# Taking out the products of the identity that TensorE does at the end of a recurrent scan

## The chip, the cores and the metric

The kernel runs on one core of a Trainium2 chip. The metric is the device time of one execution in microseconds (us); several executions are timed and their median is taken. One further execution is recorded by the hardware profiler. Times inside it are counted from the start of its span. Only the time is at stake: the change touches nothing that reaches the output.

## The reference

Two layers act on 32 sequences of 192 tokens (64 image patches and 128 text tokens) with 256 channels. Layer 0 is an embedding, causal attention and a feed-forward block with ternary weights. Layer 1 begins with a gated linear recurrence and ends with a small mixture of experts. The recurrence, cut to its core (h has 512 channels, one state for each sequence):

```python
xi, z = jnp.split(x @ Win.T, 2, axis=-1)
lam = jnp.exp(-8 * softplus(omega) * sigmoid(xi @ Wl.T + bl))
v = xi @ Wv.T + bv
def step(h_prev, inp):
    x_t, v_t, lam_t = inp
    vh = jnp.sum(v_t * h_prev, axis=-1, keepdims=True)
    vv = jnp.sum(v_t * v_t, axis=-1, keepdims=True)
    h = lam_t * (h_prev - 2.0 * v_t * (vh / vv)) + (1.0 - lam_t) * x_t
    return (h, h)
out = (silu(z) * h) @ Wout.T
```

The expert block works on 512 tokens: for each of 8 experts a 256 to 512 product, a gated activation, a 256 to 256 product and a weighted sum.

## The kernel before, in words

The program is three blocks one after the other on one core: part A (layer 0), part B (the recurrence) and part C (the experts). Between two blocks all engines meet.

Part B cuts the 192 time steps into TT = 48 tiles of four steps. Its loop runs over i from -5 to 50, and every engine has its own copy of it. In pass i the four scan steps of tile i are done (t = 4i + k, k from 0 to 3), and between them the engines work on other tiles: projections of tile i + 3, the layer norm of tile i + 5, the transposes and the output product of tile i - 1, the residual sum of tile i - 2. For i of 45 and more there are no projections left.

One scan step is a ring between two engines. VectorE (DVE) forms the products of v and the state and their sum over a partition's channels (L1219). TensorE (PE) adds these partial sums over the partitions of a sequence, with one matrix product of one column, which I call the dot (L1329, two records for each). Meanwhile VectorE multiplies the state by the decay (L1221) and adds the drive (L1224). Then it adds the dot times `B_decayed_u` (L1235), and the next step's products follow. The scan's state lives in PSUM.

TensorE's queue in pass i is: dot 0; for tiles 44 and 45 ("parted") the last nine products of `wout` (L1342, output of tile i - 2); projections; dot 1; transposes of the normalised rows of tile i + 4 (L1369, two); transposes of `B_y` of tile i - 1 (L1378, four); dot 2; projections; dot 3; `wout` of tile i - 1 (12 products, or the first three of a parted tile). The queue is in order. The transposes at L1369 wait until VectorE has done the residual sum of tile i - 2 (L1247), which needs that tile's whole `wout`.

After tile 47's scan come ScalarE's (ACT) copy of the states (L1139), GpSimd's (POOL) product with the gate (L1050), the transposes at L1378, ScalarE's L1166, VectorE's L1279, tile 47's `wout` and residual sum L1247. Then ScalarE sends four rows by a DMA, and the block ends.

Part C opens on TensorE with four transposes of the routing weights (L1603), half of expert 0's first product (`gate_up(0, ...)`, 24 products, L1573), the products of the biases (L1609, eight records) and two transposes of the last normalised rows (L1614). ScalarE and VectorE split the result (L1489, L1519), and only then can the rest of `gate_up(0)` and everything behind it go.

The identity products that the change takes out are written into TensorE's queue at two places: six after each dot of tiles 45, 46 and 47, and ten at the end of the block. They write to a PSUM bank whose contents nobody reads any more.

Of the kernel before, what the change touches and what calls it, by code (L numbers as in the profile page):

```python
# [26 lines left out]
P = 128  # L27
# [820 lines left out]
def part_b(nc, W, E, io, consts):  # L848
    TT = T // 4
    R_RES, R_RING = 12, 4  # L850
    SQRT_HALF = 0.5 ** 0.5
    with ExitStack() as ctx:
# [3 lines left out]
        ident, ones, halfpow = consts.ident, consts.ones, consts.halfpow  # L856
# [33 lines left out]
        ps = W.ps  # L890
# [4 lines left out]
        def bank(what, j):  # L895
            return (4 * j + "l v xi z".split().index(what)) % 3
# [10 lines left out]
        s = {}  # L907
# [22 lines left out]
        def products(t):  # L930
            return 4 * t + 1
# [10 lines left out]
        def has(j):  # L942
            return 0 <= j < TT
# [359 lines left out]
        def _(pe):  # L1303
# [18 lines left out]
            def step(i, k):  # L1322
                if not has(i):
                    return
                t = 4 * i + k
                if t == 0:
                    pe.wait_ge(s["minus_zero"], 8)
                pe.wait_ge(s["scan"], products(t))
                nc.tensor.matmul(dot[:, t % 2:t % 2 + 1], minus[:], part[:, t % 2:t % 2 + 1], start=True,  # L1329
                                 stop=True).then_inc(s["dot"], 1)  # L1330
                if i >= TT - 3:

                    pe.wait_ge(s["u"], TT)
                    for _ in range(6):
                        nc.tensor.transpose(ps[:, bank("v", TT - 1), 0:P], ident[:], ident[:])

            def wout(j, first, stop):
                terms = [t for g in range(IC) for t in ((y_h[:, j % 2, g, :], out_h[:, g, :]),
                                                        (y_h[:, j % 2, g, :], out_l[:, g, :]),
                                                        (y_l[:, j % 2, g, :], out_h[:, g, :]))]  # L1340
                for n in range(first, stop):
                    last = nc.tensor.matmul(ps[:, OUT, 0:D], *terms[n], start=(n == 0), stop=(n == len(terms) - 1))  # L1342
                if stop == len(terms):
                    last.then_inc(s["wout"], 1)


            parted = (TT - 4, TT - 3)
            for i in range(FIRST, LAST):
                step(i, 0)
                if i - 2 in parted:  # L1350
                    wout(i - 2, 3, 3 * IC)
                if has(i + 3):
                    j = i + 3
                    pe.wait_ge(s["x_lo"], j + 1)
                    pe.wait_ge(s["bias_l"], j + 1)
                    project(ps[:, bank("l", j), :], j, l_h, l_l, biased=True).then_inc(s["l"], 1)
                step(i, 1)
                if has(i + 3):
                    j = i + 3
# [13 lines left out]
                if has(i - 1):  # L1373
# [3 lines left out]
                    for r in range(4):  # L1377
                        last = nc.tensor.transpose(ps[:, TURN, :].rearrange("p (a r) -> p r a", r=4)[:, r, :],  # L1378
                                                   y[:, j % 2, r, :], ident[:])
                    last.then_inc(s["yT"], 1)  # L1380
                step(i, 2)
                if has(i + 3):
                    j = i + 3
# [11 lines left out]
                if has(i - 1):  # L1395
# [3 lines left out]
                    pe.wait_ge(s["y_lo"], j + 1)  # L1399
                    wait(pe, s["x_lo"], min(i + 5, TT + 3))  # L1400
                    wout(j, 0, 3 if j in parted else 3 * IC)
            for _ in range(10):
                nc.tensor.transpose(ps[:, bank("v", TT - 1), 0:P], ident[:], ident[:])


def part_c(nc, E, io, consts):
# [318 lines left out]
```

## Time and profile before

| | |
|---|---|
| median of 3 runs | 981.53 us (979.28 to 981.59) |
| the profiled execution: its time | 979.7 us |
| its span, first to last instruction | 977.8 us |
| mean granted TensorE clock | 0.993 |
| TensorE busy | 934.9 us, 96% of the span |
| VectorE busy | 791.8 us, 81% |
| ScalarE, GpSimd busy | 594.2 us, 545.2 us |
| part B's scan | 483 to 893 us |
| part C | from 901.35 us |

The profiled execution is within the runs. Its time is 1.9 us above its span. A clock of 1.00 is 2.4 GHz and 0.50 is 1.2 GHz. Matrix products are pipelined, so the time from one product's start to the next says more than a product's own duration.

### The profile page before, as it was taken

To read this page: it belongs to the slowest core of one execution; us is meant where nothing else is said; L and a number is where in the kernel's file an instruction comes from. 1 tells how busy PE (TensorE), PEld (TensorE's weight loads), DVE (VectorE), ACT (ScalarE), POOL (GpSimd) and SP (SyncE) were. 2 spreads that over 40 slices of the span, in tenths; PEclk is the share of its full clock that TensorE was granted. 3 is DMA by queue.
4 is the path that set the end of the run, shared out by engine and by line. 5 is a ranking of instruction groups with operands and counts; after the bars stand their busy time and mean duration, and the time that the engine had idled before them with its cause. 6 is when DMAs were issued, how large, how long until landed. Compare 5 with 4: busy or idle time off the path is not lost. (4 is left out here: it accounts for less than half of the span.)

```text
span 977.8 us, 19833 instructions
## 1 busy us (share of the span) xinstructions
PE 934.9 (96%) x6016; PEld 837.6 (86%) x6016; DVE 791.8 (81%) x2376; ACT 594.2 (61%) x1183; POOL 545.2 (56%) x675
## 2 busy tenths in 40 slices
PE   6889999999999999988899999999999999998998
PEld 6789999999999999875678888888888888877887
DVE  4878877777778777774589999999999989995787
ACT  1366666666666666664666767667767766752442
POOL 4256666666666666444445545455455456552673
PEclk9999999999999999999999999999999999999999
DMA  6001111111111113003799899999999999992310
GB/s 226 17 28 44 45 44 44 43 43 43 43 43 43 43 57 128 17 17 113 94 146 153 151 155 158 153 151 152 167 153 173 180 166 154 153 140 52 121 65 22
DMA packets 63014, 96.35 MB, mean 99 GB/s; under 512 B 12366, under 2 KB 32982, under 8 KB 62294
## 3 DMA queue, kind: packets, MB, share of 16 engines
q1 hardware_dynamic: 61390, 91.19, 50.1%
q0 software_dynamic: 1536, 4.20, 1.5%
q8 instruction: 37, 0.61, 0.3%
q14 instruction: 43, 0.35, 0.2%
q10 hardware_dynamic: 8, 0.00, 0.0%
HBM read 31.91 MB, written 13.11 MB: 46 GB/s over the span
## 5 line engine op out<-in xcount | busy, mean ns | idle before, releaser
L334 POOL TENSOR_TENSOR gelu_lo<-gelu_out,gelu_hi 128x384 fp32r<-128x384 f32 x124 | 146.0, 1205 | 29.2 <-DVE gelu_hi L549 28.7
L1050 POOL TENSOR_TENSOR B_y<-B_scan_in,B_states 128x512 f32<-128x512 f32 x48 | 61.8, 1288 | 84.8 <-ACT B_states L1139 84.8
L752 PE MATMUL psAB<-ternary_down,gelu_hi 128*128 128x256 f32 x384 | 96.9, 291 | 5.3 <-POOL gelu_lo L334 4.5
L688 PE MATMUL psAB<-x2T_hi,ternary_up 128*128 128x384 f32 x256 | 92.7, 362 | 0.8 <-DVE residual L678 0.6
L752 PE MATMUL psAB<-ternary_down,gelu_lo 128*128 128x256 f32 x384 | 93.4, 282 | 0.0
L688 PE MATMUL psAB<-x2T_lo,ternary_up 128*128 128x384 f32 x256 | 86.1, 336 | 0.0
L1317 PE MATMUL psAB<-Win_hi,B_x_hi 128*128 128x512 f32 x192 | 83.5, 435 | 0.0
L752 PEld LDWEIGHTS psAB<-ternary_down,gelu_hi 128*128 128x128 f32 x384 | 72.2, 188 | 9.7 <-POOL gelu_lo L334 8.0
L1062 POOL TENSOR_TENSOR B_decayed_u<-B_scan_in 128x512 f32<-128x512 f32 x48 | 62.1, 1293 | 29.5 <-DMA B_scan_in<-B_stage 28.2
L1235 DVE SCALAR_TENSOR_TENSOR psAB<-B_decayed_u,psAB 128x128 f32<-128x128 f32 x192 | 67.8, 353 | 12.1 <-PE psAB L1329 11.2
L1329 PEld LDWEIGHTS psAB<-B_partial_dots,B_minus_same_batch 128*128 128x128 f32 x384 | 65.3, 191 | 14.3 <-DVE B_partial_dots L1219 4.1
L1317 PE MATMUL psAB<-Win_hi,B_x_lo 128*128 128x512 f32 x192 | 75.5, 393 | 0.0
L1317 PE MATMUL psAB<-Win_lo,B_x_hi 128*128 128x512 f32 x192 | 75.3, 392 | 0.0
L752 PEld LDWEIGHTS psAB<-ternary_down,gelu_lo 128*128 128x128 f32 x384 | 72.5, 189 | 0.0
L1056 POOL TENSOR_TENSOR B_v_scale<-B_half_vv,half_powers 128x1 f32<-128x1 f32 x48 | 26.3, 549 | 78.8 <-ACT B_v_squared L1160 78.8
L403 ACT ACTIVATE gelu_out<-psAB 128x384 f32<-128x384 f32 x128 | 62.7, 490 | 10.2 <-PE psAB L688 9.9
L1219 DVE CUSTOM_DVE_ANT_0 B_products<-B_scan_in,psAB 128x128 f32<-128x128 f32 x192 | 55.2, 287 | 13.4 <-DVE psAB L1235 8.0
L1224 DVE TENSOR_TENSOR psAB<-psAB,B_scan_in 128x128 f32<-128x128 f32 x192 | 57.5, 299 | 6.5
L568 DVE TENSOR_TENSOR gelu_sq_sum<-gelu_sq_sum,gelu_sq 128x384 f32<-128x384 f32 x105 | 61.2, 582 | 1.7
L1329 PE MATMUL psAB<-B_partial_dots,B_minus_same_batch 128*128 128x1 f32 x384 | 54.8, 212 | 3.9 <-DVE B_partial_dots L1219 3.6
L1342 PE MATMUL psAB<-Wout_hi,B_y_hi 128*128 128x256 f32 x192 | 55.6, 290 | 2.7 <-DVE B_y_lo L1279 1.5
L390 ACT ACTIVATE gelu_sq<-gelu_out 128x384 f32<-128x384 f32 x112 | 57.3, 528 | 0.0
(274 smaller groups left out, 3318.2 us busy)
## 6 DMA issues: line engine op xcount, KB each, us to landing
B_scan_in<-B_stage SPq DMA_DIRECT2D x192, 256.0 KB, 6.9
patches<-in_patches SPq DMA_DIRECT2D x16, 384.0 KB, 3.1
B_residual<-layer_out SPq DMA_DIRECT2D x48, 128.0 KB, 4.1
out_dram<-B_residual SPq DMA_DIRECT2D x48, 128.0 KB, 3.7
layer_out<-residual SPq DMA_DIRECT2D x32, 128.0 KB, 1.8
raw_Win<-in_experts SPq DMA_DIRECT2D x3, 768.0 KB, 4.2
raw_Wl<-in_experts SPq DMA_DIRECT2D x3, 768.0 KB, 4.2
layer_out<-residual SPq DMA_DIRECT2D x32, 64.0 KB, 2.0
```

The costliest lines, as they stand in the source:

```text
L334: nc.gpsimd.tensor_tensor(act_l[:, k, :], act[:, k % DEEP, :], act_h[:, k, :].bitcast(F32), ALU.subtract).then_inc(s["ffn_lo"], 1)
L390: nc.scalar.activation(out, act[:, k % DEEP, :], ACT.Square).then_inc(s["sq_done"], 1)
L403: nc.scalar.activation(act[:, k % DEEP, :], ps[:, 6 + k % 2, 0:GT], ACT.Gelu).then_inc(s["gelu_done"], 1)
L568: nc.vector.tensor_tensor(sqsum[:], sqsum[:], sq[:, k % DEEP, :], ALU.add).then_inc(s["sqsum_done"], 1)
L688: last = nc.tensor.matmul(out, a, b, start=(n == 0), stop=(n == len(terms) - 1))
L752: last = nc.tensor.matmul(ps[:, 6 + k // 2, (k % 2) * D:(k % 2 + 1) * D], x[:, c, k * P:(k + 1) * P], dn_w[:, c, :], start=(c == 0 and x i ...
L1050: nc.gpsimd.tensor_tensor(y[:, j % 2], ring[:, j % R_RING, :, GATE, :], hs[:, j % 2], ALU.mult).then_inc(s["y"], 1)
L1062: nc.gpsimd.tensor_tensor(lu[:, j % 2], ring[:, j % R_RING, :, LAM, :], ring[:, j % R_RING, :, U, :], ALU.mult).then_inc(s["lu"], 1)
L1224: nc.vector.tensor_tensor(state(j, k), state(j, k), ring[:, j % R_RING, k, DRIVE, :], ALU.subtract).then_inc(s["scan"], 1)
L1235: nc.vector.scalar_tensor_tensor(out=state(i, k), in0=lu[:, i % 2, k, :], scalar=dot[:, t % 2:t % 2 + 1], in1=state(i, k), op0=ALU.mult, o ...
L1317: last = nc.tensor.matmul(out, a, b, start=(not biased and ks[0] == 0 and n == 0), stop=(ks[-1] == DC - 1 and n == len(terms) - 1), skip_g ...
L1329: nc.tensor.matmul(dot[:, t % 2:t % 2 + 1], minus[:], part[:, t % 2:t % 2 + 1], start=True, stop=True).then_inc(s["dot"], 1)
```

## The change

The six identity products after each scan dot of the last three tiles are removed, 72 in all, with the wait ahead of them, and so are the ten that end the block. Nothing is put in their place. VectorE's, ScalarE's, GpSimd's and SyncE's programs are unchanged.

```diff
                 pe.wait_ge(s["scan"], products(t))
                 nc.tensor.matmul(dot[:, t % 2:t % 2 + 1], minus[:], part[:, t % 2:t % 2 + 1], start=True,
                                  stop=True).then_inc(s["dot"], 1)
-                if i >= TT - 3:
-
-                    pe.wait_ge(s["u"], TT)
-                    for _ in range(6):
-                        nc.tensor.transpose(ps[:, bank("v", TT - 1), 0:P], ident[:], ident[:])
...
                     wout(j, 0, 3 if j in parted else 3 * IC)
-            for _ in range(10):
-                nc.tensor.transpose(ps[:, bank("v", TT - 1), 0:P], ident[:], ident[:])
```

## Rows read from the trace of the kernel before

**Rows 1.** The page: span, busy time of engines, granted clock in 40 slices.

```profile
span 977.8 us, 19833 instructions
PE 934.9 (96%) x6016; PEld 837.6 (86%) x6016; DVE 791.8 (81%) x2376; ACT 594.2 (61%) x1183; POOL 545.2 (56%) x675
PEclk9999999999999999999999999999999999999999
```

**Rows 2.** Chain that ended last, part C's opening: start us, us, what.

```profile
901.39 0.60 PE psC L1603 x4
901.99 2.87 PE psC L1573 x24
904.86 1.92 PE psC L1609 x8
906.78 0.38 PE psC L1614 x2
...
907.60 0.44 DVE Wl_Win_lo L1519
```

**Rows 3.** Windows from:to: length, busy us by engine, granted clock, DMA.

```profile
53.30:56.60 3.30, 3.03 (x14) 3.03 (x15) 2.02 (x9) 1.45 (x4) 0.00 (x0) 0.50 0.00 0
490.10:493.50 3.40, 1.79 (x9) 1.18 (x8) 2.47 (x10) 2.65 (x6) 2.28 (x4) 1.00 1.06 136
493.60:496.90 3.30, 3.30 (x11) 2.62 (x10) 2.52 (x8) 1.55 (x3) 1.41 (x2) 0.50 1.06 138
...
875.80:879.20 3.40, 2.30 (x18) 1.66 (x15) 3.09 (x14) 0.09 (x1) 2.47 (x5) 1.00 1.08 175
879.30:882.60 3.30, 3.30 (x18) 3.30 (x17) 1.28 (x7) 0.90 (x2) 1.28 (x1) 0.50 1.05 132
882.70:886.10 3.40, 3.26 (x29) 2.90 (x28) 3.05 (x12) 0.87 (x2) 1.28 (x1) 1.00 0.14 42
886.10:889.50 3.40, 2.89 (x25) 2.60 (x24) 2.66 (x12) 0.60 (x1) 1.29 (x1) 1.00 0.02 5
```

**Rows 4.** Source view of L1335: duration ns min/median/max, first and last start.

```profile
L1335 PE MATMUL psAB<-ident x72: 272/273/421, 872.0 to 892.7; 128*128 128x128 f32 x72
```

**Rows 5.** TensorE's timeline in the stretch of the change: start us, us, instruction.

```profile
879.17 1.47 PE L1335 MATMUL psAB<-ident 128*128 128x128 f32 x6
880.29 0.56 PE L1342 MATMUL psAB<-Wout_hi,B_y_hi 128*128 128x256 f32 x1
...
881.93 0.41 PE L1342 MATMUL psAB<-Wout_lo,B_y_hi 128*128 128x256 f32 x1
882.14 0.41 PE L1342 MATMUL psAB<-Wout_hi,B_y_lo 128*128 128x256 f32 x1
...
883.33 0.38 PE L1369 MATMUL psAB<-ident,B_normed 128*128 128x128 f32 x2
...
883.99 0.28 PE L1329 MATMUL psAB<-B_partial_dots,B_minus_same_batch 128*128 128x1 f32 x2
...
895.34 0.63 PE L1378 MATMUL psAB<-ident,B_y 128*128 128x128 f32 x4 [0.67 <-POOL B_y L1050]
...
898.95 1.25 PE L1403 MATMUL psAB<-ident 128*128 128x128 f32 x10
```

**Rows 6.** VectorE's timeline there; in brackets idle time and its releaser.

```profile
882.60 0.42 DVE L1247 SCALAR_TENSOR_TENSOR B_residual<-psAB,B_residual 128x256 f32<-128x256 f32 x1 [1.86 <-PE psAB L1342]
...
889.52 0.42 DVE L1247 SCALAR_TENSOR_TENSOR B_residual<-psAB,B_residual 128x256 f32<-128x256 f32 x1 [0.39 <-PE psAB L1342]
...
891.12 0.36 DVE L1235 SCALAR_TENSOR_TENSOR psAB<-B_decayed_u,psAB 128x128 f32<-128x128 f32 x1
```

**Rows 7.** Timelines of GpSimd and ScalarE at the end of part B and after.

```profile
893.92 1.28 POOL L1050 TENSOR_TENSOR B_y<-B_scan_in,B_states 128x512 f32<-128x512 f32 x1 [4.44 <-ACT B_states L1139]
```

```profile
899.61 1.19 ACTq L1193 DMA_DIRECT2D raw_Wv<-B_residual  x1
...
904.80 0.60 ACT L1486 ACTIVATE C_normed<-raw_Wv,C_shift,C_rstd 128x256 f32<-128x256 f32 x1 [1.94 <-POOL C_shift L1465]
```

## The prediction

> **What bounds the kernel now.** I read the page first: TensorE is busy for 96% of the span, VectorE for 81%, and the granted clock shows nines all the way [rows 1]. Taken alone this says that TensorE is the bound and that 82 fewer products are a gain. So I went on to the stretch of the change, 871.9 to 901.3 us. All 72 identity products after the dots lie there [rows 4], and the ten of the end start at 898.95 [rows 5].
>
> In that stretch no projections are left, and the scan's ring sets the pace. VectorE's timeline shows it at work except where it waits for `wout`: 1.86 us ahead of 882.60 and 0.39 us ahead of 889.52 [rows 6]. In between, an identity product mostly fills time in which TensorE would wait for VectorE's products.
>
> Then I read the chain that ended last. It reaches back to TensorE's opening of part C: four transposes, 24 products in 2.87 us, the biases in 1.92 us, two transposes, and VectorE's split at 907.60 [rows 2]. `C_normed` was there at 904.80 + 0.60 = 905.4 [rows 7], but its transposes stand in TensorE's queue behind the biases and start only at 906.78. So part C's opening is bound by TensorE, and each microsecond lost there goes straight into the end: the rest of `gate_up(0)`, and through it VectorE, ScalarE and GpSimd, begin from that split.
>
> Last I read the granted clock in windows. It is not always full. It is 0.50, that is 1.2 GHz, from 53.3, from 493.6 and from 879.3 us, each time for about 3.4 us (a fourth such spell is in part A's start). Ahead of them TensorE had little to do (1.79 us of 3.40 ahead of 493.6), in them it worked without a pause (3.30 of 3.30 at 879.3), and then the clock was full again [rows 3]. At 879.3 it fell although identities were in the queue: 875.8 to 879.2 has only 18 products in 2.30 us [rows 3]. Later, from 882.7 to 886.1, hardly anything but identities, other transposes and dots ran (29 products, 3.26 us), and the clock stayed at 1.00 in the next window too [rows 3]. So what the identities do to the time goes by two ways: the place that they take in the queue, and the clock.
>
> TensorE: Matmul & The Clock Gate, a page of the Trainium skill, says in its Part 4 (PE-mode transpose) that the full clock does not engage for transposes, since they do not count as busy time in the same way. By that rule the identities hold nothing up, and the sum below would be that of the third rival. The trace disagrees, by the two windows just named.
>
> **The change part by part.** In the new kernel TensorE has, from 871.9 us on, only dots, six transposes a tile and `wout`. I expect the clock to fall some microseconds earlier than 879.3, to come back only after the dense pieces (`wout`), and to fall again in each gap. The price of the low level: `wout`'s products start 0.21 us apart (881.93 to 882.14) [rows 5], against 2.87 / 24 = 0.12 us at full clock [rows 2]. A microsecond of dense work at the low level loses 1 - 0.12/0.215 = 0.45 us.
>
> Term 1, tile 46, step 0. Six identities stand ahead of the nine products of `wout` for tile 44, from 879.17 to 880.29 [rows 5], 1.12 us, while VectorE waits 1.86 us for the last of them [rows 6]. The nine ran at the low clock before and will after: 1.12 us gained. Ends: 1.86 us if the clock is full, 0 if something else is late. I take -1.1.
>
> Term 2, tile 46, steps 1 and 2. The residual sum now starts at 881.5 and ends at 881.9, and six transposes follow. At the low clock they take 6 x 0.215 = 1.3 us, and the dot behind them starts at 883.25 instead of 883.99 [rows 5]. The lead is 0.75 us instead of 1.1, and less by the dot's own slowness. So +0.5, between 0 (full clock) and 0.7.
>
> Term 3, tile 47, step 0. Before, six identities (0.72 us at 0.12 each) and nine products (1.06 us) lay between dot and residual sum, 1.78 us. After, nine at 0.215: 1.93 us. +0.15; ends -0.4 (the whole wait of 0.39 [rows 6]) and +0.2.
>
> Term 4, dots at the low clock. In most steps other work of VectorE covers the dot. In four steps of tiles 46 and 47 nothing lies between the drive and L1235, as at 891.12 [rows 6]. A pair of dot records takes 0.28 to 0.38 us at full clock; doubled it would cost up to 0.38 a step, nothing at the least. No row shows an uncovered dot at the low level. I take 0.1 in each of the four, +0.4, nearer the low end since a part falls at full clock; ends 0 and 1.5.
>
> Terms 1 to 4: -1.1 + 0.5 + 0.15 + 0.4 = -0.05. The scan ends where it did, which is the first point of the forecast: the identities' place in the queue and the clock cancel.
>
> Term 5, the end of part B. Tile 46's `wout` starts near 892.9: 12 products at 0.215 are 2.6 us, to 895.5. `B_y` is ready at 893.92 + 1.28 = 895.20 [rows 7] and its transposes started at 895.34 [rows 5], so 0.1 us is lost, and four slow transposes lose 4 x 0.1. Tile 47's `wout`, after this dense piece, should find the clock full. +0.5; ends 0, and 1.7 if its 12 products are low too (12 x 0.1 more).
>
> Term 6, the ten identities of the end. They run from 898.95 to 900.2 under ScalarE's issue of the DMA, 899.61 to 900.80 [rows 5, 7]. Their place is worth nothing. What they may do is hold the clock. Without them TensorE has nothing from 899.2 to 901.4, after 12 products (1.4 us) and an earlier gap of 1.5 us; the low level followed stretches with as little work as that [rows 3].
>
> Term 7, part C's opening at the low clock. The spells seen ended after some 3.4 us of dense work [rows 3]. Counted from 901.4 this gives 3.4 us, and the rise may come earlier or somewhat later by where the fall lay. I take 4.2 us x 0.45 = +1.9. Ends: 0 if the clock is full, and 24 x 0.095 + 1.92 + 0.3 = 4.5 if the products, the biases (twice their time) and the transposes all run low. I take a value nearer the middle since every spell in the rows ended by itself under dense work.
>
> Sum: -0.05 + 0.5 + 1.9 = +2.4 us. On the profiled execution 979.7 + 2.4 = 982.1. The median of the runs stands 1.8 us above that execution; the same difference on the median gives 981.5 + 2.4 = 983.9 us, or 0.24% slower.
>
> **The rivals.**
>
> First, low throughout. The clock doesn't come back before the split of part C. Term 5 becomes 1.7, term 7 becomes 4.5, the dots cost a little more: +6, 987.5 us. For it: the work from 886 to 901 is in short pieces. Against it: every low spell in the trace ended under dense work [rows 3], and 24 products in a row are dense. It decides if no rise is seen before the biases at L1609. A milder form, one spell more than I count, gives +4.
>
> Second, full clock in part C. The two `wout`s and the transposes from 892.9 on keep the clock up over the gap. Terms 1 to 5 stand, term 7 is 0: +0.5, 982.0 us. For it: in the rows the clock falls only after a stretch of little work, not at once. Against it: the gap of over 2 us follows another of 1.5 us.
>
> Third, not slower at all: the identities don't hold the clock, and only their place in the queue goes. The clock stays as before, with one low spell near 879. Gains: 1.1 at tile 46, 0.4 at tile 47 and some 0.3 of late dots, -1.8, 979.7 us (-2.7 if the spell misses `wout` as well). For it: the fall at 879.3 in spite of them. Against it: windows of identities alone, at full clock. It decides if the mean clock from 871.9 to 901.3 is no lower than before.
>
> **How the numbers follow.** The forecast case, clock low in pieces and in the opening of part C, has 0.60, with its own range +1.2 to +4.0, 982.7 to 985.5. Low throughout or one spell more: 0.15. Full clock in part C: 0.16. No hold on the clock: 0.09. The range of 980.5 to 986.5 takes in the forecast, the second rival, half of the first and some of the third. A change of 0.3%, 2.9 us, is about what a measurement of this kernel can tell. Slower by more: the upper part of the forecast case (0.29) and the first rival, 0.44. Faster by more than that needs more than the queue's place can give, 0.06. Within: 0.50.
>
> **What would show each step.** In the windows, the granted clock below 1.00 in at least two more pieces between 872 and 901, and 0.50 at the start of part C, returning before the biases end; the 24 products of its opening taking some 4.7 us instead of 2.87. VectorE's wait for `wout` in tile 46 about 0.8 instead of 1.86. The last L1235 of the scan within 0.6 us of 892.86, and part C starting 0 to 1 us later. I would be wrong if the 24 products took 2.9 us, if the scan ended over 1 us earlier or later, or if the delay at part C's split were absorbed further on.

## The result, and the profile after

| | before | changed |
|---|---|---|
| median of 7 runs each | 981.59 us (979.28 to 984.45) | 986.95 us (984.59 to 990.41) |
| profiled execution, its span | 979.7, 977.8 us | 986.9, 985.0 us |
| mean granted clock there | 0.993 | 0.977 |
| part C starts | 901.35 us | 906.12 us |

The ratio is 1.0057, 95% interval 1.0036 to 1.0077: the changed kernel is 5.4 us slower, just outside the range of 980.5 to 986.5. I forecast 983.9.

The page's clock line now shows a hole where before there were nines only [rows 1]; PE's instructions are 82 fewer and its busy time is the same.

```profile
PE 935.2 (95%) x5934; PEld 839.4 (85%) x5934; DVE 791.0 (80%) x2376; ACT 595.2 (60%) x1183; POOL 544.9 (55%) x675
PEclk9999999999999999999999999999999999975999
```

The windows of the changed kernel's trace (length, busy time and count of PE, PEld, DVE, ACT, POOL, then the granted clock) answer to [rows 3]:

```profile
871.90:876.50 4.60, 3.14 (x23) 2.77 (x24) 4.11 (x15) 1.66 (x3) 2.26 (x5) 1.00 1.07 129
876.60:881.60 5.00, 2.93 (x14) 2.50 (x13) 4.62 (x20) 1.08 (x3) 1.48 (x2) 0.50 1.07 163
881.70:886.20 4.50, 4.11 (x20) 4.02 (x20) 2.66 (x11) 0.95 (x3) 2.18 (x4) 0.50 0.97 142
886.30:891.80 5.50, 3.72 (x16) 3.67 (x17) 4.32 (x17) 1.31 (x3) 2.55 (x2) 0.50 0.02 4
891.90:895.60 3.70, 2.41 (x11) 1.90 (x10) 3.19 (x13) 0.60 (x1) 0.00 (x0) 0.50 0.11 35
895.70:899.50 3.80, 3.79 (x16) 3.38 (x16) 0.65 (x2) 0.60 (x1) 1.28 (x1) 0.50 0.02 4
899.60:903.80 4.20, 2.84 (x12) 2.63 (x12) 0.69 (x1) 2.07 (x3) 0.00 (x0) 0.50 0.22 61
903.90:907.20 3.30, 1.03 (x10) 0.99 (x10) 0.82 (x2) 1.05 (x1) 0.00 (x0) 1.00 0.01 2
907.30:910.60 3.30, 3.30 (x18) 3.30 (x17) 0.70 (x3) 0.94 (x2) 2.25 (x5) 0.50 0.83 256
...
914.20:917.40 3.20, 3.05 (x14) 3.05 (x15) 0.92 (x3) 1.59 (x2) 2.12 (x1) 0.50 0.58 230
```

From 876.6 to 903.9 us the clock is at 1.2 GHz without a break, 27.3 us. Neither the nine products of `wout` from 881.7 on (TensorE busy for 4.11 of 4.50 us) nor the 12 and four transposes from 895.7 on (3.79 of 3.80 us) brought it back. It came back at 903.9, behind tile 47's last 12, fell again at 907.3 in part C's opening and once more at 914.1, behind the split. The chain that ended last shows what that did to the opening [rows 2], 24 products in 4.36 us instead of 2.87:

```profile
906.17 0.60 PE psC L1596 x4
906.77 4.36 PE psC L1566 x24
911.13 1.92 PE psC L1602 x8
913.04 0.38 PE psC L1607 x2
...
913.87 0.43 DVE Wl_Win_lo L1512
```

VectorE's timeline, with idle time and its releaser in brackets, answers to [rows 6]:

```profile
883.96 0.42 DVE L1247 SCALAR_TENSOR_TENSOR B_residual<-psAB,B_residual 128x256 f32<-128x256 f32 x1 [0.80 <-PE psAB L1337]
...
886.36 0.36 DVE L1235 SCALAR_TENSOR_TENSOR psAB<-B_decayed_u,psAB 128x128 f32<-128x128 f32 x1 [0.84 <-PE psAB L1329]
...
892.06 0.42 DVE L1247 SCALAR_TENSOR_TENSOR B_residual<-psAB,B_residual 128x256 f32<-128x256 f32 x1 [0.80 <-PE psAB L1337]
...
893.83 0.36 DVE L1235 SCALAR_TENSOR_TENSOR psAB<-B_decayed_u,psAB 128x128 f32<-128x128 f32 x1 [0.20 <-PE psAB L1329]
...
903.93 0.42 DVE L1247 SCALAR_TENSOR_TENSOR B_residual<-psAB,B_residual 128x256 f32<-128x256 f32 x1 [3.02 <-PE psAB L1337]
```

The waits for the parted output are 0.80 us each, where they were 1.86 and 0.39.

To compare executions I cut each profile at four of VectorE's instructions: the last gate product (L1253, tile 45), the last L1235 of the scan, the last residual sum (L1247), and part C's split. The difference in span is 7.2 us. Of this, 2.3 us had arisen before the first cut (873.72 to 875.99), where both kernels run the same code; that part is how far one execution differs from another, here with the same 10.2 us of low clock ahead of the cut in both. Behind the cut it is 4.9 us, near the 5.4 us of the medians. "Low" is the time at 1.2 GHz between the first cut and the split of that one profile. "Low, timed" is the median over the timed runs, for the whole execution, worked out from each run's mean clock as 2 x (1 - clock) x span. All columns but the last two are single profiles; ratios are those of the timed runs to the kernel before on the same chip.

| run | scan | end of B | C's opening | rest | low | low, timed | ratio (95% interval) |
|---|---|---|---|---|---|---|---|
| before | 19.14 | 6.29 | 8.45 | 70.20 | 3.4 | 14 to 16 | 1 |
| changed | 19.58 | 8.36 | 9.94 | 71.13 | 30.7 | 41 | 1.0057 (1.0036 to 1.0077) |
| e1_drop_ten | 17.57 | 6.31 | 8.44 | 70.23 | 0 | 16 | 1.0009 (0.999 to 1.0027) |
| e2_keep_ten | 19.28 | 7.11 | 8.45 | 70.23 | 17.1 | 35 | 1.0034 (1.0016 to 1.0051) |
| e3_thin | 24.46 | 7.71 | 9.94 | 71.16 | 30.7 | 52 | 1.0123 (1.01 to 1.0146) |
| e4_fit | 16.55 | 6.31 | 8.46 | 71.06 | 0 | 17 | 1.0003 (0.9985 to 1.0022) |
| e5_end_only | 19.57 | 8.00 | 8.47 | 70.17 | 23.9 | 33 | 1.0038 (1.002 to 1.0056) |
| e6_three | 18.29 | 6.33 | 8.45 | 70.16 | 3.4 | 19 | 1.0017 (1.0 to 1.0035) |
| e7_changed_again | 18.81 | 8.36 | 11.07 | 71.25 | 30.7 | 47 | 1.0051 (1.0029 to 1.0074) |
| e8_twelve | 20.04 | 6.32 | 8.45 | 70.96 | 0.1 | 16 | 1.0035 (1.0018 to 1.0052) |
| e9_fit_and_c | 17.43 | 6.32 | 8.45 | 70.20 | 0 | 14 | 0.9983 (0.9969 to 0.9997) |
| e10_tile45 | 17.38 | 8.00 | 8.45 | 70.16 | 10.2 | 27 | 1.002 (1.0003 to 1.0038) |
| e11_long_piece | 18.81 | 8.25 | 8.44 | 70.98 | 17.1 | 41 | 1.0061 (1.004 to 1.0083) |
| e12_plain | 24.32 | 7.30 | 8.46 | 71.35 | 23.9 | 45 | 1.0087 (1.0067 to 1.0106) |
| e13_plain256 | 17.87 | 7.55 | 8.46 | 70.26 | 3.4 | 14 | 0.9988 (0.997 to 1.0006) |
| e14_fp32 | 17.76 | 6.32 | 8.45 | 70.22 | 0 | 18 | 1.0001 (0.9983 to 1.002) |

The timed column answers for the single profiles: no version with 14 to 19 us of low time is over 0.2% slower than before but e8_twelve, whose queue is the fullest, and every version with 27 us and more is slower, by and large the more the longer. Highest are e3_thin and e12_plain, whose fillers run at the low clock themselves.

### The profile page after: what moved, and what is told of

Its sections match the earlier page's. It is cut to its first block and busy times, and to the rows that moved or that the text cites. A ratio compares the mean times of both kernels' runs of the same rounds, so it can differ in the third digit from the quotient of the medians.

```text
span 985.0 us, 19669 instructions
## 1 busy us (share of the span) xinstructions
PE 935.2 (95%) x5934; PEld 839.4 (85%) x5934; DVE 791.0 (80%) x2376; ACT 595.2 (60%) x1183; POOL 544.9 (55%) x675
## 5 line engine op out<-in xcount | busy, mean ns | idle before, releaser
L1329 PEld LDWEIGHTS psAB<-B_partial_dots,B_minus_same_batch 128*128 128x128 f32 x384 | 67.4, 197 | 15.8 <-DVE B_partial_dots L1219 5.7
L1235 DVE SCALAR_TENSOR_TENSOR psAB<-B_decayed_u,psAB 128x128 f32<-128x128 f32 x192 | 68.0, 354 | 14.5 <-PE psAB L1329 13.7
L1062 POOL TENSOR_TENSOR B_decayed_u<-B_scan_in 128x512 f32<-128x512 f32 x48 | 61.9, 1290 | 26.5 <-DMA B_scan_in<-B_stage 17.2
L1337 PE MATMUL psAB<-Wout_hi,B_y_hi 128*128 128x256 f32 x192 | 57.9, 301 | 4.2 <-DVE B_y_lo L1279 2.0
L318 POOL TENSOR_TENSOR patches_lo<-patches,patches_hi 128x768 fp32r<-128x768 f32 x16 | 29.7, 1858 | 50.3 <-DVE patches_hi L537 50.2
```

The costliest lines, as they stand in the source:

```text
L1062: nc.gpsimd.tensor_tensor(lu[:, j % 2], ring[:, j % R_RING, :, LAM, :], ring[:, j % R_RING, :, U, :], ALU.mult).then_inc(s["lu"], 1)
L1235: nc.vector.scalar_tensor_tensor(out=state(i, k), in0=lu[:, i % 2, k, :], scalar=dot[:, t % 2:t % 2 + 1], in1=state(i, k), op0=ALU.mult, o ...
```

## The experiments

My theory: the identities act through the clock; the changed kernel is slow because TensorE runs at 1.2 GHz. The rivals: it is their place in the queue, or the wait for `u` that goes with the 72; or only one of the two places matters.

**Which of the two places.** e1_drop_ten takes only the ten out, e2_keep_ten only the 72.

```diff
-            for _ in range(10):
-                nc.tensor.transpose(ps[:, bank("v", TT - 1), 0:P], ident[:], ident[:])
```

> Only the ten identity products of the block's end are taken out; the 72 between the dots stay. Clock theory: the scan and the end of part B are as before; TensorE has no work in the 2.2 us before part C, so its opening runs partly at 1.2 GHz, +0.7 to +1.9 us on the whole time. Rival, that the ten are worth nothing because 1.4 us of dense work stand just ahead of the gap: 0, the 24 products of the opening take 2.9 us as before.

Measured: 982.08 against 981.26 us. Its windows show the whole stretch at full clock:

```profile
875.70:905.00 29.30, 22.53 (x178) 19.45 (x177) 19.65 (x73) 8.47 (x14) 8.77 (x10) 1.00 0.44 73
```

The opening takes 8.44 us as before. So with the 72 in place the ten do nothing that can be seen, and the rival of this run is the one that the profile bears out. The timed runs alone, with an interval from 1.0 us faster to 2.6 us slower, wouldn't decide between the two expectations; their median low time, 16 us, is that of before.

The edit of e2_keep_ten:

```diff
-                if i >= TT - 3:
-
-                    pe.wait_ge(s["u"], TT)
-                    for _ in range(6):
-                        nc.tensor.transpose(ps[:, bank("v", TT - 1), 0:P], ident[:], ident[:])
```

> Only the 72 identity products between the dots are taken out; the ten at the end stay. Clock theory: the clock is low from about 876 to the end of part B as in the changed kernel, the scan loses 0.4 us and the end of part B 2 us; the ten, run at the low clock just ahead of part C, bring the rise forward, so that part C loses less than the changed kernel's 2.4 us: +3 to +4.5 us in all. Rival, that all of the loss comes from the 72: +5 us or more. Rival, that the ten carry it: under +2 us.

Measured: 985.02 us, 3.8 more than before (981.26), within the first expectation. Low for 17.1 us in this profile, with one return to 2.4 GHz between; the opening is at full clock. The 72 carry most of the loss. What the ten add to it is not settled: the intervals of this run and of the changed kernel overlap.

**The changed kernel again**, with its spread.

> The changed kernel once more, beside the others on this chip: +4 to +6 us. Its low spells should begin within a few microseconds of 876 again; the long one of 27 us may be broken into pieces, as the changed kernel's products fall otherwise against the moments at which the clock changes, and the time of the stretch follows how much of it is low.

Measured: nine runs, 988.89 us median, 981.92 to 989.71. By the medians that is 7.6 us more than the 981.28 of before beside it, by the ratio 5 us; five of the nine lie near 989, four between 982 and 984.5. Each timed run lists its mean clock, and time follows it: 981.92 us at 0.986, 984.33 at 0.981, 989.03 at 0.974. From 2 x (1 - clock) x span the low time is 27 to 55 us in these runs (median 47) and 10 to 26 (median 14) in the 29 of before beside them. A line through the nine gives 0.29 us of time for each microsecond at the low level (correlation 0.95), through the changed kernel's first seven runs 0.23 (0.94). 27 to 33 us more (41 or 47 less 14) at 0.23 to 0.29 would be 6 to 10 us; the medians are 5.4 and 7.6 us apart, somewhat less. The places in the queue that the change frees may account for the difference; no run shows it. In this profile the clock came back only at 913.5, 0.1 us ahead of the biases at 913.63, and the opening, with 8.1 us of low clock, took 11.07.

**The scan alone, the end alone.** e5_end_only has identities only behind the scan, e10_tile45 only behind the dots of tile 45 (and the ten). The edit of e5_end_only, against the kernel before:

```diff
+                if i == TT:
+                    fill(4)
                 if has(i - 1):
...
                     last.then_inc(s["yT"], 1)
+                    if i == TT:
+                        fill(10)
...
-            for _ in range(10):
-                nc.tensor.transpose(ps[:, bank("v", TT - 1), 0:P], ident[:], ident[:])
+            fill(14)
```

(`fill(n)` is n identity transposes into the same bank; the 72 are out, the wait for `u` ahead of them stays.)

> The 72 between the dots are taken out; identity products stand only behind the scan: four ahead of the last transposes of the states, ten behind them, 14 at the end. Clock theory: the scan runs at the low clock and loses what the changed kernel loses there, 0.4 us against the profile of before and up to 2 against one without a low spell; the rest fills TensorE from 895 on, so the clock is back before part C and its opening takes 2.9 us for 24 products: +1.5 to +3.5 us. Rival, that the loss is all in the scan: +5. Rival, that it is all behind the scan: 0 within 1 us.

Measured: 984.96 against 981.28 us. The clock came back only at 903.5 of this profile, ahead of part C, whose opening is at full speed. The loss is 3.7 us, a little more than the 1.5 to 3.5 I expected. The scan and the end of B lose about as in the changed kernel (19.57 and 8.00 against 19.58 and 8.36). Since the wait for `u` stands in this run and the scan takes the same as without it, the wait itself costs nothing.

The edit of e10_tile45:

```diff
-                if i >= TT - 3:
+                if i == TT - 3:
```

> The six identity products are kept behind the dots of tile 45 only, where VectorE is the bound, and the ten at the end are kept. Clock theory: the clock falls about one tile later than in the changed kernel, then the same: tiles 46 and 47 low, the scan 18.3 to 19.5 us from the last gate product (17.6 at full clock with all 72), the block's end 7 to 8.4; +2.5 to +4.5 us. If it is only a first fall that the identities prevent: the clock full to the end, and -1 us.

Measured: 982.24 against 980.80 us, less than I expected. In the profile the clock fell at 887.3 for 3.4 us and at 894.1 for 6.8 us: one spell is in the scan, which takes 17.38 us, and the rest slows the block's end to 8.00. By the ratios, 1.002 against 1.0034 of e2_keep_ten, the 24 of tile 45, which stand where VectorE is the bound, save a good third of the loss; the intervals overlap, so this is the likelier reading and no more. The median low time of the timed runs, 27 us against 35, points the same way.

**How many.** e6_three and e8_twelve put three and twelve in place of six; the edit of e6_three:

```diff
-                    for _ in range(6):
+                    for _ in range(3):
```

> Three identity products after each dot of the last three tiles instead of six; the ten at the end stay. Clock theory: less work than in the kernel before, so one or two low spells more between 875 and 893, and less of the queue taken: +0.5 to +3 us, VectorE's waits for the parted output 0.1 to 0.4 us where the clock is full. If three hold the clock as well as six: -0.5 to -1 us.

Measured: 982.55 against 981.28 us, at the edge of the interval. This profile, like that of before, has one low spell of 3.4 us in the scan, which takes 18.29 us. The median low time is 19 us against 14: three hold the clock nearly as well as six.

> Twelve identity products after each dot instead of six. The queue holds 1.4 us of them after each dot, the ring of dot and VectorE needs as little as 1.3 us a step: the clock is full from 872 into part C, and the dots and the parted output come late, VectorE waits 1.1 us and more for the latter: +3 to +6 us. If identity products give way to other work or cost nothing in the queue: 0.

Measured: 983.69 against 981.28 us, 2.4 more, where I expected 3 to 6. The clock is full through scan and opening, and the scan takes 20.04 us, 2.5 more than with six at full clock (e1_drop_ten). VectorE's timeline shows the price of the queue's place:

```profile
883.39 0.42 DVE L1247 SCALAR_TENSOR_TENSOR B_residual<-psAB,B_residual 128x256 f32<-128x256 f32 x1 [1.04 <-PE psAB L1342]
...
891.52 0.42 DVE L1247 SCALAR_TENSOR_TENSOR B_residual<-psAB,B_residual 128x256 f32<-128x256 f32 x1 [1.05 <-PE psAB L1342]
```

Without the ten, with six behind each dot and at full clock too (e1_drop_ten), these two waits are 0.40 us each. So both ways of the prediction are real, with opposite signs.

**What kind of work holds the clock.** In place of each six identity transposes: three fp32 products of one column (e3_thin), six ordinary fp32r products of 128 columns (e12_plain, its edit below), the same of 256 (e13_plain256: `0:2 * P` for the output and the second operand), three ordinary fp32 products of 128 columns (e14_fp32: `ident[:]` for both operands, `range(3)`). An fp32 product has two records, so three of them are six records too. The edit of e12_plain:

```diff
-                        nc.tensor.transpose(ps[:, bank("v", TT - 1), 0:P], ident[:], ident[:])
+                        nc.tensor.matmul(ps[:, bank("v", TT - 1), 0:P], in_h[:, 0, 0:P], in_h[:, 0, 0:P], start=True, stop=True)
```

The edit of e3_thin:

```diff
-                    for _ in range(6):
-                        nc.tensor.transpose(ps[:, bank("v", TT - 1), 0:P], ident[:], ident[:])
+                    for _ in range(3):
+                        nc.tensor.matmul(ps[:, bank("v", TT - 1), 0:1], ident[:], ident[:, 0:1], start=True, stop=True)
```

(and five of them for the ten at the end)

> In place of each six identity products stand three fp32 products of one column (six weight loads of 128 columns, six one-column records, some 0.7 us of the queue), and five in place of the ten. If the columns that TensorE works through hold the clock: low from about 876 on as in the changed kernel, and about +5 us or somewhat more, since the queue is as full as before. If an occupied queue with its weight loads is enough: clock and time as before, 0 within 1.5 us.

Measured: 993.37 against 981.26 us, 12.1 more; I had expected the low clock, but only about 5 us for it. A window of its trace shows TensorE occupied without a pause, and the clock low:

```profile
880.00:900.00 20.00, 20.00 (x96) 20.00 (x97) 11.21 (x46) 2.93 (x6) 5.95 (x8) 0.50 0.36 55
```

This also separates the two ways: the queue holds as many records as before, the clock is as in the changed kernel, and the time is worse than either, since the fillers too take twice their time (they start 0.21 us apart from 878.5 on, 0.11 us before).

> The 72 transposes of the identity become 72 ordinary fp32r products of the same 128 columns (Win_hi with itself); the ten at the end stay. If a transpose holds the clock as an ordinary product does: low time and time as before, 0 within 1.5 us, plus what the product's own duration adds. If transposes count for less: fewer low spells than before, none near 879, -0.5 to -1.5 us.

Measured (four runs): 990.79 against 980.80 us. Neither of the two expectations: I had not thought that ordinary products could hold less than transposes. Windows of its trace:

```profile
885.00:890.00 5.00, 5.00 (x26) 5.00 (x25) 2.58 (x11) 1.05 (x2) 1.27 (x1) 0.50 0.75 94
890.00:895.00 5.00, 5.00 (x25) 5.00 (x25) 3.10 (x13) 0.87 (x2) 1.26 (x1) 0.50 0.08 26
895.00:900.00 5.00, 5.00 (x25) 5.00 (x25) 2.17 (x9) 0.60 (x1) 1.28 (x1) 0.50 0.02 3
900.00:905.00 5.00, 5.00 (x26) 5.00 (x25) 2.91 (x12) 1.20 (x2) 0.05 (x1) 0.50 0.08 26
```

TensorE: Matmul & The Clock Gate, of the Trainium skill, advises in its closing part (Why this matters for your kernels) to keep TensorE busy continuously to reach the full clock. These windows show that it doesn't hold for every kind of work: TensorE is busy for 20 us of 20 and stays at 1.2 GHz.

> Six ordinary fp32r products of 256 columns, twice those of the run with 128, in place of each six identity transposes; a product of either width takes 0.12 us of the queue at full clock. If what counts is how much TensorE streams, not that it is occupied: low time as in the kernel before or less, 0 within 1.5 us. If ordinary products hold the clock less than fp32 transposes whatever their width: low from about 883 on, +8 to +11 us.

Measured: 981.08 against 982.51 us. The profile has one low spell, from 898.7 to 902.2, in the block's end. Windows of its trace in the scan:

```profile
880.00:885.00 5.00, 4.60 (x37) 4.21 (x36) 4.11 (x17) 1.09 (x2) 2.75 (x6) 1.00 1.06 127
885.00:890.00 5.00, 4.57 (x35) 3.98 (x34) 4.17 (x16) 1.47 (x3) 1.73 (x2) 1.00 0.50 65
890.00:895.00 5.00, 4.93 (x41) 4.60 (x40) 4.16 (x17) 0.89 (x2) 0.84 (x1) 1.00 0.08 26
```

The source views of the two runs show that at full clock a product takes nearly the same whichever its width (272 ns the shortest of e12_plain, 277 here):

```profile
L1335 PE MATMUL psAB<-Win_hi x72: 272/415/454, 877.8 to 904.7; 128*128 128x128 f32 x72
```

```profile
L1335 PE MATMUL psAB<-Win_hi x72: 277/282/372, 874.7 to 894.3; 128*128 128x256 f32 x72
```

Six of them in a row at full clock, first e12_plain's, then those of this run, take 0.86 and 0.96 us on TensorE's timelines:

```profile
877.82 0.86 PE L1335 MATMUL psAB<-Win_hi 128*128 128x128 f32 x6
```

```profile
874.71 0.96 PE L1335 MATMUL psAB<-Win_hi 128*128 128x256 f32 x6
```

So the queue of e13_plain256 is if anything the fuller one, and yet its scan takes 17.87 us against 24.32. The two runs take their operands from the same tensor and differ in the width alone, and the intervals of their ratios (0.997 to 1.0006 and 1.0067 to 1.0106) lie far apart. It is the cleanest evidence that the loss comes through the clock.

> Three ordinary fp32 products of the identity, 128 columns and two records each, in place of each six fp32 transposes. If an fp32 operand is what makes the work count: low time and time as before, 0 to +2 us. If it is the transpose: low from about 880 on, +6 us and more.

Measured: 982.55 against 982.51 us, no low time from the first cut on. So it is not the transpose as such that holds the clock, and a transpose doesn't count for nothing either: 128 columns of fp32 held it in both forms, 128 columns of fp32r did not, 256 of fp32r did. The fp32 runs multiply the identity and the fp32r runs `Win_hi`, so what the type does and what the values do is not told apart. The statement of the Trainium skill on transposes, which the prediction weighed (TensorE: Matmul & The Clock Gate, Part 4), is not borne out for fp32 ones.

**What brings the clock back.**

> All 82 are taken out and 14 put in at one place, right behind tile 47's 12 products of the second last output, so that TensorE has 26 products in a row. If uninterrupted work brings the clock back: low from about 876 to about 900, tile 47's last output and part C's opening at full clock for the most part; the 14 delay the last transposes by 2 to 3 us and give back 1.2 and up to 1.5: +4 to +6 us, part C's opening 8.5 us. If a length of dense work doesn't matter: low until part C, +7 to +9 us.

```diff
+                if i == TT:
+                    fill(14)
                 if has(i - 1):
```

(The 82 of before are out.)

Measured: 986.36 against 980.80 us. The clock had come back once on its own between two low pieces, from 885.6 to 889.0, and again at 899.22, inside the 26 products; the opening is at full speed. The whole is as slow as the changed kernel: the end of B takes 8.25 us, as the 14 delay the transposes behind them. The time is in the range I expected, but not by what I built the run for. TensorE's timeline has the last of the 12 output products at 898.90 and the first of the 14 at 899.11:

```profile
898.90 0.41 PE L1346 MATMUL psAB<-Wout_hi,B_y_lo 128*128 128x256 f32 x1
899.11 1.75 PE L1326 MATMUL psAB<-ident 128*128 128x128 f32 x14
```

So the rise came 0.1 us into the first identity, when hardly more had run than the 12 products that the changed kernel has there too, and the run doesn't show that the length of the piece brought it. That length alone is not enough is shown by e12_plain's 20 us.

**Identities by the gaps.** e4_fit spares the places where something waits for the queue; e9_fit_and_c has six more in part C. Against the changed kernel e4_fit has:

```diff
+            FILL = ((6, 6, 10, 10), (0, 3, 6, 10), (0, 3, 6, 6))
...
+                if i >= TT - 3:
+                    pe.wait_ge(s["u"], TT)
+                    fill(FILL[i - (TT - 3)][k])
```

(and the `fill(4)`, `fill(10)`, `fill(14)` of e5_end_only; one row of `FILL` for each of tiles 45 to 47, one number for each step)

> Identity products are kept but placed by the gaps: none ahead of the parted output products (step 0 of tiles 46 and 47), three instead of six after step 1 of those tiles, ten where TensorE waits longest (after steps 2 and 3 of tile 45, step 3 of tile 46), four ahead of and ten behind the last transposes of the states, 14 at the end. Clock theory: the clock stays full from 872 into part C, VectorE's waits of 1.86 and 0.39 us shrink to under 0.3 each, -1 to -2.5 us against the kernel before. Rival, that the low spell at 879 comes anyway: -0.5 to -1.5. If the queue's places don't matter: 0.

Measured: 981.03 against 981.26 us, nothing that can be told, where I expected 1 to 2.5 us less. The scan is the shortest of all, 16.55 us, and VectorE doesn't wait for the parted output. In this profile a low spell fell into part C at 909 and cost 0.9 us in the rest (71.06 against 70.2).

What e9_fit_and_c has besides:

```diff
                 last = nc.tensor.transpose(ps[:, 7, c * P:(c + 1) * P], xn[:, c * P:(c + 1) * P], ident[:])
             last.then_inc(s["xT"], 1)
+            for _ in range(6):
+                nc.tensor.transpose(ps[:, 2, MT // 2:MT // 2 + P], ident[:], ident[:])
```

> The placement by gaps as in the run before it with 14 at the end, and six more identity products in part C behind its last transposes, in the 0.9 us in which TensorE waits for VectorE's split. Clock theory: no low spell between 872 us and the end, the scan 16.6 us from its last gate product as before in that placement, part C after the split 70.2 us; -0.5 to -2 us against the kernel before, at the edge of what the runs can tell. If the low spells are not governed by TensorE's gaps: a spell after 905 in the profile, and 0.

Measured: 979.96 against 980.80 us, ratio 0.9983, 95% interval 0.9969 to 0.9997. It is the fastest version, by a margin at the edge of the measurement against before and, by the two ratios to before, which come from different chips, some 0.7% ahead of the changed kernel (0.9983 / 1.0057). Its scan took 17.43 us in the profile, not 16.6, 0.9 us more than e4_fit's. VectorE's timeline says why: two waits go back to one transfer, the second through GpSimd's L1062, which itself had waited for it (4.30 us, until 887.95). There the transfer is the next bound:

```profile
887.84 0.29 DVE L1219 CUSTOM_DVE_ANT_0 B_products<-B_scan_in,psAB 128x128 f32<-128x128 f32 x1 [0.56 <-DMA B_scan_in<-B_stage]
...
889.26 0.36 DVE L1235 SCALAR_TENSOR_TENSOR psAB<-B_decayed_u,psAB 128x128 f32<-128x128 f32 x1 [0.58 <-POOL B_decayed_u L1062]
```

## Why the prediction was wrong

The sign and the mechanism held. The step that failed is the sentence on the clock: that it would "come back only after the dense pieces (`wout`), and to fall again in each gap". I had read off the spells before that each ended under dense work after some 3.4 us, and took any `wout` for such work. In the changed kernel the clock stayed low through two dense pieces, 27.3 us in one, and that made the end of part B cost 2.07 us instead of the 0.5 of term 5. The second thing that failed is the end that I set to the change's reach: a further spell behind the split, which stands in no term, cost 0.93 us. The milder form of the first rival is what came, and in e7_changed_again's profile its full form but for 0.1 us, the rise just ahead of the biases; the rival had 0.15 for both its forms, which was too little.

Term by term, in the profiled execution:

- Terms 1 to 4, the scan. Term 1: VectorE's wait went from 1.86 to 0.80, 1.06 gained (1.1 forecast). Term 2: the dot behind the slow transposes came late by 0.84 instead of 0.22, +0.62 (+0.5). Term 3: 0.80 instead of 0.39, +0.4 (+0.15). Term 4: three uncovered dots were waited for 0.20 to 0.24 us, and these steps are 0.15 to 0.17 us longer each, +0.47 (+0.4). Sum +0.44, measured 19.58 - 19.14 = +0.44; forecast -0.05.
- This small number hides a choice: the profile of before happened to have a low spell at 879. The same scan at full clock is 17.57 us (e1_drop_ten), so against an execution without a spell the changed kernel's scan loses 2.0 us. The sum was made against one profile with a spell; how many executions of before have one there isn't on record.
- Term 5, the end of part B. +0.5 forecast, 8.36 - 6.29 = +2.07 measured. Tile 47's `wout` ran at the low level too; I had 1.7 as the highest price of that end, which was too low as well. Part C came 2.5 us later from the first cut, where I had 0 to 1 as the sign to look for.
- Term 6. That the ten are worth nothing by their place is right: part C starts 2.2 us after the last residual sum in both. That they are needed to hold the clock for part C was wrong as long as the 72 are there (e1_drop_ten).
- Term 7, the opening. +1.9 forecast, 9.94 - 8.45 = +1.49 measured, and 11.07 - 8.45 = +2.6 in the other profile. The size was near, the pattern not: in the first profile the clock was full at the start and fell inside, in the other it was low from before the start.
- Not in the sum: a further low spell behind the split, 914.1 to 917.5, +0.93 in the rest. I had ended the change's reach at the split.

Together 0.44 + 2.07 + 1.49 + 0.93 = 4.9 us against 2.4: 0.5 more in the scan, 1.6 more in term 5, 0.4 less in term 7, and 0.9 of the spell behind the split. The third rival is refuted: with the identities gone the low time went up from 3.4 to 30.7 us, and in the timed runs from a median of 14 to one of 41 to 47. That each microsecond lost in the opening goes into the end is borne out: the rest of part C takes 70.2 us in all profiles without a low spell behind the split.

What stays open: why the clock came back once inside the scan in e2_keep_ten, e7_changed_again and e11_long_piece and not in the changed kernel's first profile. The products are the same and stand at nearly the same places; I have no run that tells it apart.

## What to carry to other kernels

A product that computes nothing can be worth its place when it keeps TensorE's clock up in a stretch that is bound by a ring with another engine; judge it by two prices, what stands behind it in the queue and what the low level costs up to the next stretch that TensorE bounds. Put such products where TensorE waits anyway, none ahead of work that another engine waits for (what that gave over the kernel before is at the edge of what the runs can tell), and look at the granted clock and not at the busy time to see whether they do their work. Compare low time over all timed runs before summing against one profile: one low spell more or less is 0.8 to 1.6 us here (0.8 in e8_twelve's part C, 1.57 in the scan of before against e1_drop_ten).

## What the runs showed of the hardware that I had not expected

- TensorE without a pause for 20 us and at 1.2 GHz all the while, with fp32r products of 128 columns as fillers (e12_plain), and likewise with one-column fp32 products (e3_thin). With 256 columns of fp32r (e13_plain256), at the same place in the queue, the clock was full in the scan.
- A low piece can be long: 3.4 us in every spell of before's profile, 23.9 to 27.3 us in one piece in both profiles of the changed kernel and in three experiments (e3_thin, e5_end_only, e12_plain).
- Two executions of the same code differ before they reach the change: the last gate product of tile 45 starts between 873.7 and 879.6 us in the profiles, with 10.2 to 20.5 us of low clock ahead of it. Such a spread limits what a measurement of this kernel can tell.
